# RWKV token mixing: four low-rank products as one, a tile ahead, the decay product last, the gate's Silu after the lag stage, and the scans between the first pair products

## What is computed

```python
sx = _shift(x) - x
xxx = x + sx * p['x_maa']
mix = jnp.tanh(xxx @ p['tm_w1']).reshape(b * t, 5, E)            # E = 32
mix = jnp.einsum('nfe,fed->fnd', mix, p['tm_w2'])                # five low-rank products
wx, kx, vx, rx, gx = (x + sx * (p[n + '_maa'] + m) ...)
r = jax.nn.sigmoid(rx @ p['Wr'])
k = kx @ p['Wk']
v = vx @ p['Wv']
g = jax.nn.silu(gx @ p['Wg'])
w = jnp.tanh(wx @ p['td_w1']) @ p['td_w2']
w = jnp.exp(-jnp.exp(p['time_decay'] + w))
out = _wkv(r4, k4, v4, w, p['time_first'])                       # recurrence over the tokens
out = group_norm(out) * p['gn_w'] + p['gn_b']
return out * g @ p['Wo']
```

## Time and profile before

| | |
|---|---|
| median of 3 runs | 8399.8 us (8382.2 to 8408.21) |
| the profiled execution | 8404.84 us |
| its span in the profile | 8403.0 us |
| mean granted TensorE clock | 0.917 |
| TensorE (PE), busy | 7087.1 us |
| VectorE (DVE), busy | 6290.8 us |
| ScalarE (ACT), busy | 2611.7 us |
| GpSimd (POOL), busy | 3076.4 us |

### The profile page before, as it was taken

The page is one execution under the profiler, slowest core; times in us unless marked ns, Lnnn a source line. Parts: engine busy times, 40 slices in busy tenths (PEclk is TensorE's granted clock), DMA queues, the critical chain, the costliest instruction groups (busy, mean ns, idle before and its releaser), DMA issues. The chain is left out here.

```text
span 8403.0 us, 239054 instructions
## 1 busy us (share of the span) xinstructions
PE 7087.1 (84%) x91097; PEld 4097.0 (49%) x91097; DVE 6290.8 (75%) x14037; ACT 2611.7 (31%) x5021; POOL 3076.4 (37%) x3870
## 2 busy tenths in 40 slices
PE   5999999999973834887886799999999999999997
PEld 3666666666621312253252455555555555555554
DVE  8777777777758476496585678788788887888876
ACT  2111111111142322403404334444444444343444
POOL 1333333333300000030120556565555555555653
PEclk7999999999986866788788999999999999999999
DMA  0000000000000000000001311121211111121112
GB/s 21 1 1 1 0 1 0 1 0 1 0 5 1 4 13 0 0 1 1 0 1 47 101 53 58 52 58 55 60 54 56 56 54 56 54 63 52 58 52 65
DMA packets 156920, 242.83 MB, mean 29 GB/s; under 512 B 21616, under 2 KB 136848, under 8 KB 150160
## 3 DMA queue, kind: packets, MB, share of 16 engines
q1 hardware_dynamic: 155920, 228.84, 9.0%
HBM read 187.06 MB, written 13.66 MB: 24 GB/s over the span
## 5 line engine op out<-in xcount | busy, mean ns | idle before, releaser
L2800 POOL TENSOR_TENSOR big<-big 128x512 f32<-128x512 f32 x388 | 495.9, 1278 | 1767.5 <-DVE big L2638 1653.0
L2810 POOL TENSOR_TENSOR big<-big 128x512 f32<-128x512 f32 x776 | 1081.3, 1424 | 16.9 <-DMA big<-norms 1.9
L834 POOL TENSOR_TENSOR big<-big 128x128 f32<-128x128 f32 x1024 | 415.3, 406 | 1336.8 <-DVE big L780 1336.5
L2202 PE MATMUL banks<-hidden,big 128*128 128x256 f32 x3104 | 813.5, 400 | 74.0 <-DMA hidden<-big 36.2
L600 ACT ACTIVATE banks<-banks 128x128 f32<-128x128 f32 x1024 | 268.3, 262 | 1821.0 <-DVE banks L763 1821.0
L1901 POOL TENSOR_TENSOR big<-big 128x448 f32<-128x448 f32 (+10 forms) x160 | 158.2, 992 | 1841.8 <-ACT big L1656 1710.7
L334 PE MATMUL banks<-big,weights_even 128*128 128x512 f32 (+5 forms) x1152 | 623.1, 694 | 233.3 <-DVE big L1086 45.1
L2266 PE MATMUL banks<-big,hidden 128*32 128x512 f32 x6144 | 784.8, 603 | 0.0
L489 PE MATMUL banks<-big 128*128 128x256 f32 x2050 | 730.1, 438 | 61.9 <-ACT big L574 59.5
L2202 PEld LDWEIGHTS banks<-hidden,big 128*128 128x128 f32 x3104 | 559.1, 192 | 393.1 <-issue 85.3
L2245 PE MATMUL banks<-big 32*32 32x64 f32 (+1 forms) x49152 | 635.7, 223 | 132.5 <-issue 132.1
(11 more groups left out here) (357 smaller groups left out, 13875.2 us busy)
## 6 DMA issues: line engine op xcount, KB each, us to landing
big<-norms SPq DMA_DIRECT2D x776, 128.0 KB, 2.9
big<-qk SPq DMA_DIRECT2D x50, 512.0 KB, 4.8
big<-vo SPq DMA_DIRECT2D x25, 1024.0 KB, 5.8
weights_odd<-ffn SPq DMA_DIRECT2D x25, 537.5 KB, 4.4
hidden<-big SPq DMA_DIRECT2D x171, 64.0 KB, 3.6
hidden<-big SPq DMA_DIRECT2D x25, 256.0 KB, 3.0
hidden<-big SPq DMA_DIRECT2D x25, 255.8 KB, 3.7
big<-pairs SPq DMA_DIRECT2D x6, 1024.0 KB, 11.1
```

The source lines that it names most:

```text
L834: nc.gpsimd.tensor_tensor(full(u["kS"][s % 2]), full(S), by(u["ko_c"]), ALU.mult).then_inc(*e.did(("kS", s)))
L2202: mm = self.nc.tensor.matmul(bank[:, n * QTOK:(n + 1) * QTOK], u["w" + name.lower()][:, (2 * g + n) * P:(2 * g + n + 1) * P], u["xs"][:, a ...
L2800: self.nc.gpsimd.tensor_tensor(dst, cos, sin, ALU.add).then_inc(*e.did(("turned_pair", f, name, g)))
L2810: self.nc.gpsimd.tensor_tensor(x, x, u["norms"][:, n, g].unsqueeze(1).broadcast_to([P, 2, QTOK]), ALU.mult).then_inc(*e.did(("scaled", f, ...
```

## The change

- **Low-rank products.** tm_w1 is applied as one product of 128 columns (w, k, v, r) and one of 32 (g), into two banks. ScalarE applies one Tanh to each. The result of the first has four groups of 32 partitions, so tm_w2 is stored with its first four blocks stacked on the partitions, and the products of w, k, v, r use array rows 0 to 31, 32 to 63, 64 to 95, 96 to 127. g uses rows 0 to 31.
- **A tile ahead.** tm_w1 and Tanh of tile t+1 are issued after tile t's tm_w2 products, in two alternating places of `b[7]`. The mixed inputs have four slots, in rotation over all tiles.
- **Decay product last.** td_w2 comes after Wg.
- **Tables.** The set of Sigmoid is loaded ahead of the loop. The output of Wg is written by Copy; Silu is applied to it in four pieces after the chunk decays, and the gate waits for it.
- **Scans.** They follow the pair products 1, 3, 5, 7; the sums come after entries 9, 12, 15, 18. The mask is in `b[1]`. GpSimd's products for d = 2 also wait for the pair product of d = 1 of their tile.
- `weights_even` has at least 5120 columns.

```diff
-        w[f"{r}tm_w2"] = g("tm_w2").transpose(1, 0, 2).reshape(32, 5 * P)
+        w[f"{r}tm_w2"] = np.concatenate([g("tm_w2")[:4].reshape(P, P), np.concatenate(
+            [g("tm_w2")[4], np.zeros((P - 32, P), np.float32)])], axis=1)
...
+def mix_view(b, t, f):
+    k = 2 * (t % 2) + f // 4
+    return b[7][:, k * TILE:(k + 1) * TILE]
+
+def mixed_view(b, t, f):
+    k = 4 + (5 * t + f) % 4
+    return b[7][:, k * TILE:(k + 1) * TILE]
...
 def rwkv_tensor(core, e):
+        def mixes(t):
+            pe.wait_ge(*e.after(f"{r}xxx", t))
+            core.product(e, core.to_act, [(w(r, "tm_w1", 0, P), b[2][:, tok(t)])])
+            core.product(e, core.to_act, [(w(r, "tm_w1", P, 32), b[2][:, tok(t)])], rows=32)
+
+        mixes(0)
         for t in range(TILES):
-            pe.wait_ge(*e.after(f"{r}xxx", t))
+            pe.wait_ge(*e.after(f"{r}mix", t))
             for f in range(5):
-                core.product(e, core.to_act, [(w(r, "tm_w1", 32 * f, 32), b[2][:, tok(t)])], rows=32)
-            for f, (name, _) in enumerate(MIXED):
-                pe.wait_ge(*e.after(f"{r}mix", t, f))
-                core.product(e, core.to_dve, [(w(r, "tm_w2", P * f, P), b[7][0:32, f * TILE:(f + 1) * TILE])])
+                rows = slice(32 * (f % 4), 32 * (f % 4) + 32)
+                core.product(e, core.to_dve, [(w(r, "tm_w2", P * (f // 4), P)[rows], mix_view(b, t, f)[rows])])
+            if t + 1 < TILES:
+                mixes(t + 1)
             for f, (name, _) in enumerate(MIXED):
                 pe.wait_ge(*e.after(f"{r}xf", t, f))
-                x = b[7][:, (5 + f % 3) * TILE:(6 + f % 3) * TILE]
+                x = mixed_view(b, t, f)
                 if name == "w":
                     core.product(e, core.to_act, [(w(r, "td_w1"), x)], rows=64)
-                    pe.wait_ge(*e.after(f"{r}tdtanh", t))
-                    core.product(e, core.to_act, [(w(r, "td_w2"), sm[0:64, 0:TILE])])
                 else:
                     core.product(e, core.to_act, [(w(r, "W" + name), x)])
+            pe.wait_ge(*e.after(f"{r}tdtanh", t))
+            core.product(e, core.to_act, [(w(r, "td_w2"), sm[0:64, 0:TILE])])
...
 def rwkv_scalar(core, e):
+        nc.scalar.preload_act_table(ACT.Sigmoid)
+
+        def mixes(t):
+            for part, rows in enumerate((P, 32)):
+                bank, label = core.drain(e, core.to_act)
+                if t >= 2 and part == 0:
+                    act.wait_ge(*e.after(f"{r}xf", t - 2, 4))
+                nc.scalar.activation(mix_view(b, t, 4 * part)[0:rows], bank[0:rows, :], ACT.Tanh).then_inc(*e.did(label))
+            alias((f"{r}mix", t), label)
...
-                    func = {"r": ACT.Sigmoid, "g": ACT.Silu}.get(name, ACT.Copy)
+                    func = ACT.Sigmoid if name == "r" else ACT.Copy
...
+        for s in range(BATCH):
+            nc.scalar.activation(b[5][:, seq(s)], b[5][:, seq(s)], ACT.Silu).then_inc(
+                *e.did(f"{r}gates" if s == BATCH - 1 else None))
...
 def rwkv_vector(core, e):
-                if f >= 3:
-                    dve.wait_ge(*e.after(f"{r}xf_used", t, f - 3))
-                elif t:
-                    dve.wait_ge(*e.after(f"{r}xf_used", t - 1, f + 3 if f < 2 else 2))
+                if 5 * t + f >= 4:
+                    dve.wait_ge(*e.after(f"{r}xf_used", *divmod(5 * t + f - 4, 5)))
...
-        mask = core.wbuf[1][:, 0:SEQ]
+        mask = b[1][:, 3 * SEQ:4 * SEQ]
...
-        for s in range(BATCH):
-            nc.vector.tensor_tensor_scan(C[:, seq(s)], mask, X[:, seq(s)], 0.0, ALU.mult, ALU.add).then_inc(*e.did())
-        chain()
+
+        def scan_of(s):
+            nc.vector.tensor_tensor_scan(C[:, seq(s)], mask, X[:, seq(s)], 0.0, ALU.mult, ALU.add).then_inc(
+                *e.did((f"{r}scanned", s)))
...
-            if i in (4, 8, 12, 16):
-                sums_of(i // 4 - 1)
+            if i in (1, 3, 5, 7):
+                scan_of(i // 2)
+            if i in (9, 12, 15, 18):
+                sums_of(i // 3 - 3)
...
+        dve.wait_ge(*e.after(f"{r}gates"))
...
 def rwkv_pool(core, e):
+            pool.wait_ge(*e.after(f"{r}pair", LAG_OF[d - 1, group[-1]]))
             if d == 2:
                 pool.wait_ge(*e.after(f"{r}fade", group[0] // 2))
             else:
-                pool.wait_ge(*e.after(f"{r}pair", LAG_OF[d - 1, group[-1]]))
```

More of the change, by code:

```diff
@@ L1631, in rwkv_scalar @@
         core.norm_act(e, f"{r}ln1", b[0], b[1], (f"{r}copied",), "eps5")
-        for t in range(TILES):
-            for f in range(5):
-                bank, label = core.drain(e, core.to_act)
-                if f == 0 and t:
-                    act.wait_ge(*e.after(f"{r}xf", t - 1, 4))
-                nc.scalar.activation(b[7][0:32, f * TILE:(f + 1) * TILE], bank[0:32, :], ACT.Tanh).then_inc(*e.did(label))
-                alias((f"{r}mix", t, f), label)
+        nc.scalar.preload_act_table(ACT.Sigmoid)
[6 more added lines that the diff above has]
+            alias((f"{r}mix", t), label)
+        mixes(0)
+        for t in range(TILES):
+            if t + 1 < TILES:
+                mixes(t + 1)
             for f, (name, _) in enumerate(MIXED):
                 bank, label = core.drain(e, core.to_act)
-                out = b[OUTS[name]][:, tok(t)]
                 if name == "w":
```

12 lines of the change are left out of this document (7 added, 5 removed).

## The result

| | before | after |
|---|---|---|
| median of 4 runs | 8398.06 us (8382.2 to 8408.21) | 8269.11 us (8261.72 to 8273.95) |
| the profiled execution | 8404.84 us | 8273.95 us |
| mean granted TensorE clock | 0.917 | 0.925 |

The ratio is 0.9847, with a 95% interval of 0.983 to 0.9865: 129 us faster. I had forecast 8258, with a range of 8240 to 8300. The sign and the mechanism of the loops held; in the lag stage, half of the gain came from a place that I hadn't costed. The gain was forecast at 147 us and is 131 between the profiled executions: the loops gave 12 less than forecast, the lag stages 4 more, and stretches that the change doesn't touch took 8.5 more.

A forecast was written before the change was run, and what follows sets the result against it. TensorE's own queue was taken to bound the mixing loops. From 8404.84 us, -142.7 for the two loops and -4 for the scans gave 8258 us, range 8240 to 8300.

The forecast's parts named there:

- What bounds the loop: Mixing loop: TensorE's own queue sets the pace, 20.0 us a tile before, with a falling clock and two serial waits.
- Overlap of row groups: Mixing loop: four tm_w2 products on four row groups run at once, 0.96 us instead of 3.4.
- Rival 1: Mixing loop: row groups do not overlap and the clock falls in many tiles; 12.5 us a tile, 8292 us; chance 0.13.
- The serial order of a tile: Mixing loop: TensorE's products in their new order take 10.3 us a tile, VectorE close behind.
- The clock stays at 1.0: Mixing loop: with narrow rows working four at a time, TensorE's clock stays at 1.0, against a mean of 0.75 before.
- Rival 2: Mixing loop: overlap, but the clock still falls every tile; about 13.3 us a tile, +42, 8300 us; chance 0.10.
- Start and first tile: Mixing loop: 4.4 us for two tm_w1 and a Tanh, then 14 for a first tile partly at the low clock.
- 6.86 us of VectorE idle behind two table loads: Mixing loop before: VectorE idles 6.86 us until the next tile's first tm_w2, behind last outputs, two table loads, five Tanh.
- rival 3: Mixing loop: two table loads a tile stay, partly covered, +1 us each tile; 8274 us; chance 0.03.
- The lag stage: Scans spread between pair products, GpSimd waiting: -2 us a layer, bounds +3 and -6, -4 for two.
- At nothing: Gate's Silu in ScalarE's 41.64 us idle, Sigmoid preload, moved mask and later sums: all costed at zero.
- The sum: Whole kernel: 8404.84 less 142.7 for the loops and 4 for the scans gives 8258 us.

The follow-up runs named there:

- experiment 5: Kernel after with td_w2 moved back behind td_w1, ahead of Wk: 8257.41 us, loops 102.94 and 103.03.
- experiment 6: Kernel after with tm_w1 and its Tanh at the start of their own tile, not a tile ahead: 8286.79 us, loops 114.14 and 114.27.
- experiment 11: Kernel after reordered: next tile's four tm_w2 before Wg, fifth behind tm_w1, td_w2 before Wg, one shape for single products: 8225.75 us.
- experiment 2: Kernel after with the first four tm_w2 products zero-padded to all 128 rows, run one after the other: 8280.74 us.
- experiment 8: Kernel after with td_w1 and the second tm_w1 widened to 128 columns, td_w2 to 128 rows: 8242.31 us.
- experiment 4: Kernel after with four scans back to back before the pair products and sums at their old places; GpSimd's new wait kept: 8263.7 us.
- experiment 10: Kernel after without GpSimd's new wait for its d = 2 products, scans still between pair products: 8261.76 us.
- experiment 1: Kernel after with merging undone: five 32-column tm_w1 products, five Tanh, five tm_w2 products on one row group: 8322.95 us.
- experiment 9: Kernel before with the table part alone added: Sigmoid set preloaded, Copy for g, Silu behind the chunk decays: 8390.34 us.
- experiment 3: Kernel after with Silu back in the loop and no Sigmoid preload, so two table loads a tile: 8269.49 us.
- experiment 7: Kernel after with the fifth tm_w2 product moved behind the next tile's tm_w1: 8243.06 us.

## Why the prediction was right, and where its sizes were off

**What bounds the loop: right.** TensorE's queue, with the clock and two waits. Experiments 5, 6 and 11 changed nothing but its order (11 the shapes too) and moved the loop by +5.7, +17 and -15.6 us.

**Overlap of row groups: right.** I took 0.96 us, the next product can begin after 1.07. Experiment 2 took the overlap away and the tile grew by 1.67 us. Rival 1 (no overlap, 8292 us) fell; its 12.5 us a tile is close to the 12.40 of that experiment, but the clock stayed up there.

**The serial order of a tile: right in every step, 4% short.** The fifth product at 1.96 us (2.0), td_w2's end at 10.73 (10.3). The mis-sized term is the change of shape, 0.1 us in the prediction. By the timeline a lone product of a new shape takes 0.98 to 1.06 us instead of 0.86 to 0.96, and the four W products take 3.63 instead of 3.50. By experiment 8 a change is worth 0.14 us. Step by step: fifth product +0.09, tm_w1 +0.15, td_w1 +0.05, the W products +0.13, td_w2 +0.05, the start -0.04, so 0.43 us a tile and 2.6 in the six tiles that have it in full.

**"The clock stays at 1.0": nearly right.** It fell once a loop, from 77.0 to 80.4 us after its start in both, and that tile took 12.36: 1.6 us. With the same loop code it also fell twice, in the second loops of experiments 4 and 10. Rival 2 (a fall in every tile, 8300 us) fell with it. Experiment 1 shows that the danger was real: with five products alone on one row group the clock fell seven times a loop. Without the tile ahead (experiment 6) it fell twice, for 6.8 us each.

**Start and first tile: short.** 4.6 us (4.4) and 15.5 (14). The low clock lasted until 15.5 us after the start of the loop. The sum of a loop is now 4.6 + 15.5 + 77.2 = 97.3 against 4.4 + 14 + 73.0 = 91.4.

**"6.86 us of VectorE idle behind two table loads": wrong as a reading.** The loads stood in the list of what VectorE waited through, but the wait is 6.68 without them (experiment 9), and putting them back in after costs nothing a tile (experiment 3). In the timeline of experiment 9 what lies there is TensorE's five tm_w1 products with a Tanh behind each, 0.86 us apart, and then the first tm_w2 product. The number wasn't harmed, since the sum was built from TensorE's queue, and rival 3 (loads remain, 8274) would have cost about 1 us and not 16. To name what a wait was for, look at the instruction that ended it and not at what lies within it.

**The lag stage: right in sign, half the size, and the other half was not in the sum.** Forecast -2 a layer pass, measured -3.9 and -4.5, within the bounds of +3 and -6. All that I had costed lies in the first part of the stage, which gained 2.2 us in the first pass (86.47 to 84.27) and 2.9 in the second, so there the size was nearly right. Its terms were less so. Two fast scans were forecast and came, at 2.28 us, and the other two took 2.87 and 2.90 and not 3.18. Against that, the two pair products that met a GpSimd product cost 1.4 us more together, where I had given back 0.8. The term that I had left out is what GpSimd's new wait does further on: -2.7 us at the turn between the halves, +1.05 in the rest (experiment 10). The prediction looked at GpSimd's products for d = 2 only where they begin, at the scans, and the same four come again in the second half.

The late scans had begun when 0.72 and 0.75 us of a GpSimd product were left, and were 0.6 longer; the pair product of 1.42 us had 0.91 left and was 0.79 longer. The Trainium skill, SBUF — State Buffer, section "SBUF: two separate sides", says that a VectorE operation with two inputs in SBUF and a GpSimd operation that reads SBUF share a pair of ports as a lock and not as a bandwidth: whichever starts first keeps it for its whole instruction, and the other waits. The trace agrees as far as it goes: GpSimd's four products, which started first, took 1.17 us each, and VectorE's weighing products, of whose two inputs one is in a PSUM bank, took 50.6 us a stage before and 50.5 in after. By that rule the cost of a meeting is about what is left of the other's instruction, which is how I should have costed it.

**At nothing:** Silu, the Sigmoid preload, the mask and the later sums cost nothing that can be seen: ScalarE idles 31.59 us behind the Silu.

**The sum.** Loops -131.0 (forecast -142.7), lag stages -8.4 (-4), untouched code +8.5 (0): -130.9 (-146.7). The first two errors have opposite signs and leave 7 us, so part of the closeness is luck. The third is nothing that a prediction of this change could hold: such stretches differ by 8 to 20 us between the 13 profiles, and why their clock is higher in some is open. The forecast's own span, 8242 to 8272, holds the median of the runs, 8269.11, and not the profiled execution, 8273.95.

## What to carry to other kernels

Products with few rows belong on different row groups: four then held TensorE for 1.07 us, as long as one, and they don't stand alone in a line, which is where the clock fell most here. (Each of the four wrote to a bank of its own; one bank for all was not tried.) When TensorE's own queue is the limit, write down the time of each product in it, look for every one that waits for something just issued, and put another in its place: here that order was worth 17 and 5.7 us of a loop in the change, and another 15.6 behind it. Table loads, busy shares and long waits of the other engines say little as long as that queue isn't held by them; try such a part alone before giving it a share of a gain. When an engine is made to wait, follow it through the whole stage: what GpSimd's wait was meant for gave 0.4 us beside the spread scans, what it did 80 us later gave 2.7, and behind that it cost 1.1.

## What was unexpected of the hardware

- A change of shape between products costs 0.14 us on average (experiment 8). It paid to widen three products, of 32 columns, 64 columns and 64 rows, to the full shape, with results that nobody uses: 10.16 against 10.73 us a tile.
- With one product moved by one place (experiment 7, one run) the full clock came 7 to 12 us earlier in the loop and its one fall was gone. That was worth more than the wait that the edit removed. Loops with the very code of after differed by 3 us and one fall.
- A VectorE scan of 1024 columns takes 2.27 us alone and up to 3.25 beside GpSimd's products; these take 1.17 us when they start first and took 2.90 to 3.14 in the run of before, where each met a scan. A pair product of 64 columns takes 0.27 us alone and 1.28 beside them.
- The same code for the chunk states takes 88.7 to 98.9 us, with mean clocks of 0.88 to 0.76, and differs between two passes of one run (98.91 and 91.99). What decides it wasn't tried.
